# Routing and the last down products of a four-stage layer stack on one core: choice on logits, down products by tile, routing interleaved

## What is computed

```python
logits = x @ gate_w.T                        # [2048, 64]
probs = softmax(logits)
w, sel = top_k(probs, 8); w = w / sum(w)
pos = rank of the token among those that chose the same expert, in order of tokens
valid = pos < 128                            # at most 128 rows for an expert
out = silu(rows @ wg) * (rows @ wu) @ wd     # for each expert, on its rows
y[token] += w * out                          # for valid choices
```

## Time and profile before

| | us |
|---|---|
| three runs | 1732.64, 1737.85, 1740.98 |
| their median | 1737.85 |
| the profiled execution | 1744.28 |
| its span, from the first to the last instruction | 1742.4 |
| outside its span | 1.9 |
| TensorE busy in the span | 1506.9 (86%) |
| VectorE busy | 1062.9 (61%) |
| ScalarE busy | 583.2 (33%) |
| POOL busy | 794.6 (46%) |

### The profile page before, as it was taken

The page is one execution under the profiler, slowest core; times in us unless marked ns, Lnnn a source line. Parts: engine busy times, 40 slices in busy tenths (PEclk is TensorE's granted clock), DMA queues, the critical chain, the costliest instruction groups (busy, mean ns, idle before and its releaser), DMA issues. The chain is left out here.

```text
span 1742.4 us, 19092 instructions
## 1 busy us (share of the span) xinstructions
PE 1506.9 (86%) x5792; PEld 1038.0 (60%) x5792; DVE 1062.9 (61%) x1591; ACT 583.2 (33%) x1034; POOL 794.6 (46%) x491
## 2 busy tenths in 40 slices
PE   6989966899948899988999899999991799998992
PEld 2444323577736677766887787778771455554551
DVE  4887688887898987889988746452553122222220
ACT  4434633344534335343433322121210232222220
POOL 3467853354744445634644326662376232222222
PEclk8999988999969999999999999999995899999996
DMA  6899663356644677766655468997760799999987
GB/s 202 251 280 277 194 217 132 101 156 196 199 140 149 201 221 222 216 192 225 187 183 169 145 201 305 351 317 227 227 191 25 227 329 317 311 306 301 307 211 126
DMA packets 193541, 380.41 MB, mean 218 GB/s; under 512 B 20994, under 2 KB 95106, under 8 KB 192944
## 3 DMA queue, kind: packets, MB, share of 16 engines
q1 hardware_dynamic: 165360, 322.89, 59.8%
q0 software_dynamic: 20032, 39.92, 9.7%
q10 hardware_dynamic: 8064, 16.55, 2.8%
HBM read 301.65 MB, written 124.35 MB: 244 GB/s over the span
## 5 line engine op out<-in xcount | busy, mean ns | idle before, releaser
L1453 POOL TENSOR_TENSOR y<-y,hc 128x2048 f32<-128x2048 f32 x64 | 293.3, 4582 | 250.3 <-DVE hc L1295 250.3
L590 PE MATMUL bank<-tokT,ring 128*128 128x512 f32 x768 | 307.9, 401 | 12.9 <-DVE xall L1150 6.9
L1277 DVE TENSOR_TENSOR_SCAN bx<-bank,state,bx 128x512 f32<-128x512 f32 x256 | 312.6, 1267 | 0.8
L592 PE MATMUL bank<-tokT,ring 128*128 128x512 f32 x768 | 302.3, 394 | 0.0
L591 PE MATMUL bank<-tokT,ring 128*128 128x512 f32 x768 | 302.2, 393 | 0.0
L940 ACT ACTIVATE bank<-dl,an 128x512 f32<-128x512 f32 x256 | 171.0, 684 | 330.4 <-DVE bx L1277 330.3
L1459 POOL TENSOR_TENSOR act<-th,act 128x512 fp32r<-128x512 f32 x96 | 126.4, 1316 | 269.6 <-ACT act L864 269.1
L819 PE MATMUL bank<-wgu,xeT 128*128 128x384 f32 x512 | 181.0, 498 | 0.0
L590 PEld LDWEIGHTS bank<-tokT,ring 128*128 128x128 f32 x768 | 146.2, 190 | 49.2 <-issue 17.6
L602 PE MATMUL bank<-ring,act 128*128 128x512 f32 x360 | 147.6, 410 | 22.6 <-DVE th L1139 17.3
L592 PEld LDWEIGHTS bank<-tokT,ring 128*128 128x128 f32 x768 | 146.0, 190 | 32.1
(11 more groups left out here) (147 smaller groups left out, 2007.9 us busy)
## 6 DMA issues: line engine op xcount, KB each, us to landing
ring<-w_all SPq DMA_DIRECT2D x288, 512.0 KB
wgu<-wgu_in SPq DMA_DIRECT2D x64, 768.0 KB
wde<-wd_in SPq DMA_DIRECT2D x64, 384.0 KB
slots<-empty_in SPq DMA_DIRECT2D x16, 1154.0 KB, 8.7
w_all<-staged_u SPq DMA_DIRECT2D x64, 256.0 KB, 3.2
xe<-slots ACTq DMA_DIRECT2D x56, 288.5 KB
w_all<-fst SPq DMA_DIRECT2D x48, 256.0 KB, 3.7
w_all<-staged_d SPq DMA_DIRECT2D x32, 256.0 KB, 3.7
```

The costliest lines, as they stand in the source:

```text
L590: nc.tensor.matmul(b[:, :], w[:, k, 0, :], x[:, 0, k, :], start=(k == 0), stop=False)
L592: last = nc.tensor.matmul(b[:, :], w[:, k, 1, :], x[:, 0, k, :], start=False, stop=(k == KT - 1))
L1277: nc.vector.tensor_tensor_scan(bx[:, k, :], dA[k % 2][:, :], bx[:, k, :], state[:, k, n:n + 1], ALU.mult, ALU.add).then_inc(S_sc, 1)
L1453: nc.gpsimd.tensor_tensor(y[c % 2][:, :, :], y[c % 2][:, :, :], hc[:, :, :], ALU.add).then_inc(S_ya, 1)
```

## The change

It consists of five edits.

1. **Choice on logits.** VectorE takes the 8 largest logits (`max`), negates the first of them for the exp's bias, replaces the 8 in a copy by a very small number, and makes the mask from that, first in bf16 for the place product (which now waits for step 4 instead of 10). ScalarE makes two exps: of the 8 chosen logits with their sum, and of all 64. The weight is exp x (1 / sum) x mask in one instruction. The key of a slot is position + first slot + 2,000,000 for a chosen expert, with 1,000,000 more where the expert is full, so that one `max` and one subtraction give the slot numbers; `RS` is 14.
2. **Low half of the last mixer on VectorE** instead of POOL, two positions after the up quantum as before.
3. **Held weights.** The down weights of blocks 0 and 1 go to a buffer `held` of their own (over `spr`), loaded by SP at TURN+14 after the last transposes of the mixer. They leave the ring, so the six ring buffers end with blocks 2 to 7, and the last of these loads waits for the last up quantum.
4. **Down products by tile.** `tail(t, js)` does all 8 blocks for one tile, so `TAIL` is two positions earlier, and routing and scatters of tiles 8 to 11 are one position earlier (`base+5` for the scatters of tiles 0 to 11).
5. **The tail is written out** on each engine: the routing of a tile stands between two halves of the products of the next, and POOL's roots stand between scatters.

```diff
             with ExitStack() as last_products:
+                held = sb(last_products, "held", [P, 2, 2 * D], f32r)
-            RS = 17
+            RS = 14
...
+            HELD = M1 - RING
+            quanta = [q for q in quanta if q not in [(len(HALVES) - 1, "down", j) for j in range(HELD)]]
...
-            TAIL_FROM = M1 - RING
-            TAIL = TURN + 12 + 2 * M1 + TAIL_FROM
+            TAIL = TURN + 12 + 2 * M1
...
-            route_at = [DRAIN + 12 + 5 * i for i in range(EARLY)] + [TURN + 13 + 4 * i for i in range(TT)] + [TAIL + 1 + i for i in range(TT)]
+            route_at = [DRAIN + 12 + 5 * i for i in range(EARLY)] + [TURN + 12 + 4 * i for i in range(TT)]
...
                         if pos == TURN + 14:
+                            sp.wait_ge(n3.tp, TT * NCH)
+                            for j in range(HELD):
+                                sp.dma_start(held[:, j, :].bitcast(fp32), a["w_all"][3 * tile_of(len(HALVES) - 1, j) + 2]).then_inc(S_held, 16)
                             load_weights(4, 4)
...
-                    def tail(t):
+                    def tail(t, js):
...
-                        for j in range(TAIL_FROM, M1):
-                            w = ring_ready((h, "down", j)).rearrange("p (s h) -> p s h", s=2)
+                        for j in js:
+                            if j < HELD:
+                                pe.wait_ge(S_held, 16 * HELD)
+                                w = held[:, j, :]
+                            else:
+                                w = ring_ready((h, "down", j))
...
                     def place(i):
-                        pe.wait_ge(S_r, RS * i + 10)
+                        pe.wait_ge(S_r, RS * i + 4)
...
+                    first_part, second_part = range(M1 // 2), range(M1 // 2, M1)
+                    place(11)
+                    tail(0, range(M1))
+                    tail(1, first_part)
+                    route_T(12)
+                    tail(1, second_part)
+                    logits(12)
+                    tail(2, first_part)
+                    place(12)
+                    route_T(13)
+                    tail(2, second_part)
+                    logits(13)
+                    tail(3, first_part)
+                    place(13)
+                    route_T(14)
+                    tail(3, second_part)
+                    logits(14)
+                    route_T(15)
+                    place(14)
+                    logits(15)
+                    place(15)
...
-                        nc.scalar.activation(rt[:, 0, :], HB[2][:, 0:E], ACT.Exp, bias=rc[:, 1:2], accum_out=rc[:, 2:3]).then_inc(S_ex, 1)
+                        nc.scalar.activation(rt[:, 6, 0:TOPK], top8[:, 0, :], ACT.Exp, bias=rc[:, 1:2], accum_out=rc[:, 2:3])
+                        act.wait_ge(S_r, RS * i + 3)
+                        nc.scalar.activation(rt[:, 0, :], HB[2][:, 0:E], ACT.Exp, bias=rc[:, 1:2]).then_inc(S_ex, 1)
...
+                    def gated_lo(h, j):
...
+                        dve.wait_ge(S_gt, i + 1)
+                        dve.wait_ge(S_ah, i + 1)
+                        nc.vector.tensor_tensor(act8[:, 1, j, :], th[:, i % 2, :], act8[:, 0, j, :].bitcast(fp32),
+                                                ALU.subtract).then_inc(S_al, 1)
...
                             dve.wait_ge(S_lg, i + 1)
+                            nc.vector.max(top8[:, 0, :], logit).then_inc(S_r, 1)
                             after(1)
+                            nc.vector.tensor_scalar(rc[:, 1:2], top8[:, 0, 0:1], -1.0, None, ALU.mult).then_inc(S_r, 1)
+                            nc.vector.match_replace(rest, top8[:, 0, :], logit, TAKEN).then_inc(S_r, 1)
+                            after(3)
+                            nc.vector.tensor_scalar(chosen_b[:, :], rest, TAKEN / 2, None, ALU.is_lt).then_inc(S_r, 1)
+                            nc.vector.tensor_scalar(chosen, rest, TAKEN / 2, None, ALU.is_lt).then_inc(S_r, 1)
+                            after(5)
+                            nc.vector.tensor_tensor(first, chosen, first_slot[:, :], ALU.mult).then_inc(S_r, 1)
+                            nc.vector.tensor_copy(r[:, ROW - 1:ROW], number[:, :]).then_inc(S_r, 1)
+                            dve.wait_ge(S_ex, i + 1)
+                            nc.vector.reciprocal(rc[:, 3:4], rc[:, 2:3]).then_inc(S_r, 1)
+                            after(8)
+                            nc.vector.scalar_tensor_tensor(out=r[:, D:D + E], in0=rt[:, 0, :], scalar=rc[:, 3:4], in1=chosen,
+                                                           op0=ALU.mult, op1=ALU.mult).then_inc(S_r, 1)
                         else:
+                            dve.wait_ge(S_pm, i + 1)
+                            nc.vector.tensor_tensor(key, position, first, ALU.add).then_inc(S_r, 1)
+                            nc.vector.tensor_scalar(far, position, float(CAP), FAR, ALU.is_ge, ALU.mult).then_inc(S_r, 1)
+                            after(11)
+                            nc.vector.tensor_tensor(key, key, far, ALU.add).then_inc(S_r, 1)
+                            after(12)
+                            nc.vector.max(top8[:, 1, :], key).then_inc(S_r, 1)
+                            after(13)
+                            nc.vector.tensor_scalar(idx[:, i % SLOTS, :], top8[:, 1, :], -BASE, None, ALU.add).then_inc(S_r, 1)
...
+                    def finished(i):
+                        if i >= 3 * TT:
+                            down_added(len(HALVES) - 1, [i % TT])
+                        dve.wait_ge(S_de, TT * x3_half[i // TT] + i % TT + 1)
+                        stats(n4, i % TT, xall[:, i // TT])
...
+                    side(TAIL)
+                    route(11, 2)
+                    side(TAIL + 1)
+                    finished(12)
+                    route(12, 0)
+                    finished(13)
+                    route(12, 1)
+                    route(13, 0)
+                    route(12, 2)
+                    finished(14)
+                    route(13, 1)
+                    route(14, 0)
+                    route(13, 2)
+                    finished(15)
+                    route(14, 1)
+                    route(15, 0)
+                    route(14, 2)
+                    route(15, 1)
+                    route(15, 2)
...
-                            if kind == "up":
+                            if kind == "up" and h < len(HALVES) - 1:
                                 gated_lo(h, j)
...
+                    for k in range(3):
+                        rows_out(11, k)
+                    rstd(12)
+                    for k in range(3, TOPK):
+                        rows_out(11, k)
+                    rstd(13)
+                    rows_out(12, 0)
+                    rows_out(12, 1)
+                    rstd(14)
+                    for k in range(2, TOPK):
+                        rows_out(12, k)
+                    rstd(15)
+                    for i in range(13, 16):
+                        for k in range(TOPK):
+                            rows_out(i, k)
```

More of the change, by code:

```diff
@@ L30 @@
 FAR = 1.0e6
+BASE = 2.0e6
+TAKEN = -3.0e38
 EPS = 1e-5
@@ L1047, in _ @@
                         states(c)
-                    for pos in range(DRAIN, LAST):
+                    for pos in range(DRAIN, TAIL):
                         side(pos)
@@ L1183, in side @@
                                 down_added(h)
+                        for h, kind, j in quanta_at.get(pos - 2, ()):
+                            if h == len(HALVES) - 1 and kind == "up":
+                                gated_lo(h, j)
                     def split_x_lo(c, b):
@@ L1303, in route @@
                         r = row[:, i % SLOTS, :]
-                        pr, rest, chosen, key, v = (rt[:, j, :] for j in range(1, 6))
+                        rest, chosen, first, key, far = (rt[:, j, :] for j in range(1, 6))
+                        logit, position = HB[2][:, 0:E], HB[3][:, 0:E]
                         def after(s):
-                            dve.wait_ge(S_const, 1)
                             dve.wait_ge(S_r, RS * i + s)
@@ L1346, in route @@
-                            nc.vector.scalar_tensor_tensor(out=v, in0=HB[3][:, 0:E], scalar=float(CAP), in1=chosen,
-                                                           op0=ALU.is_lt, op1=ALU.mult).then_inc(S_r, 1)
-                            after(13)
-                            nc.vector.tensor_tensor(key, key, v, ALU.mult).then_inc(S_r, 1)
-                            after(14)
-                            nc.vector.max(top8[:, 1, :], key).then_inc(S_r, 1)
-                            after(15)
@@ L1353, in route @@
-                            nc.vector.tensor_scalar(top8[:, 2, :], top8[:, 1, :], 0.0, FAR, ALU.is_equal, ALU.mult).then_inc(S_r, 1)
-                            after(16)
-                            nc.vector.scalar_tensor_tensor(out=idx[:, i % SLOTS, :], in0=top8[:, 1, :], scalar=-1.0, in1=top8[:, 2, :],
```

(2 more changed lines are left out.)

92 lines of the change are left out of this document (41 added, 51 removed).

## The result

The changed kernel takes 1721.33 us (median of 6 runs, 1717.19 to 1724.62), the kernel before 1735.94 in the same comparison. The ratio is 0.9915, interval 0.9891 to 0.9938: 14.6 us or 0.85% faster, by the prediction's bound of 0.5% a gain. One of the six runs of before took 5255.45 us; the median of the other five is 1734.03, and the gain by it 12.7. The profiled executions differ by more, 1744.28 against 1721.55. To see why, I cut each span at four events: the first logits (tile 0), the first down product of the last mixer (the T of the prediction), the first scatter of tile 12, and the load of expert rows. "Stage" is from the first logits to that load, which is all that the change touches; "tail" is from T to the load.

A forecast was written before the change was run, and what follows sets the result against it. TensorE's place waits bound the routing, tile 12's slot numbers and then POOL's scatter rate the tail. Part 1's -10.6 and Parts 2 to 4's -11.5 made -22.1 us, so 1716 us against the median, range 1708 to 1729.

The forecast's parts named there:

- Part 1: Routing, choice on logits: all 11.0 us of TensorE's place waits go, 0.4 given back, -10.6 us.
- Part 2: Last mixer, low half on VectorE: POOL no longer falls behind; VectorE's 8 x 0.68 us covered by idle time.
- Part 3: Held down weights: no ring wait; the last down block's load lands at 3.9 us, needed at 4.9.
- Part 4: Tail's down products by tile: last scatter ends 62.1 us after the last up product; Parts 2 to 4 -11.5 us.
- The sum: Whole kernel: -10.6 and -11.5 added to -22.1 us, 1716 us against the median.
- A late semaphore falls into the chain: Rival, between the last up product and tile 12's first scatter: a late release is uncovered; 1722 to 1725 us, chance 0.10.
- DMA: Rival, early routing stretch: DMA binds once TensorE's waits are gone; 1720 to 1725 us, chance 0.15.
- Port exclusion: Rival, routing beside scatters: VectorE steps and scatters exclude each other, 6.9 us a tile; 1747 us, chance 0.05.
- Load to end: From the load of expert rows to the end: 386 us, its length independent of when it starts.

The follow-up runs named there:

- place_late: Changed kernel with the place product waiting for step 9 (weights in the row) instead of step 4 (mask); ratio to before 0.9880.
- after_third: Changed kernel, unchanged file, profiled a third time; 1713.6 us, ratio to before 0.9870.
- low_on_pool: Changed kernel with the low half of the last mixer back on POOL; 1724.85 us, ratio to before 0.9919.
- choice_only: Kernel before with the choice on logits alone added; 1728.28 us, ratio to before 0.9934.
- after_again: Changed kernel, unchanged file, profiled a second time; ratio to before 0.9905.
- runs_broken: Changed kernel with a one-column addition on POOL behind every second scatter of tiles 8 to 11; ratio to before 0.9876.
- tail_only: Changed kernel with the routing of the kernel before and the low half on POOL; ratio to before 0.9942.

## Why the prediction was right, and where it was not

The forecast was 1716 us (22.1 less), the result 1721.3 and 14.6 less; the direction and the range (1708 to 1729) hold.

- **Part 1 (-10.6)** is right in kind and under-sized: -12.3 to -12.6 to T where nothing takes it back, since a stand costs more than its wait. The earlier release alone gave nothing (place_late). In the changed kernel's own profile only 7.0 were left at T: late deliveries, through late rows and the clock behind them, gave back most of the rest.
- **Part 2 (no cost, an end to the backlog)** was right in what it said of the two engines, and its cost of nothing is still the term that failed in two of three profiles. The backlog went: tile 10's last scatter ends at T + 1.9 in after_third and at T + 5.4 in low_on_pool, and the tail is 62.8 against 66.0. The cover on VectorE held: without late deliveries T comes at 225.5 with 0.2 us of waits on the row, and in choice_only, with the subtractions on POOL, at 225.2. What the part had at nothing is what the subtractions did among POOL's scatters. Without them rows of six and more stand in the last mixer, and late deliveries in five of six profiles: alone the part costs 12.2 us, about all of it by late deliveries. On top of the other parts it saves 5.2 us (293.4 to 288.2, on two chips) without them, 0.2 the wrong way (293.6) on the chip of low_on_pool, and costs 2.3 (295.7) in the first profile. A late row costs TensorE more than the stand, as it may then run at 0.66 to 0.72 of its clock.
- **Part 3 (no cost)** held without late deliveries: no ring wait. With them the last load is issued 2.5 us late and TensorE stands 1.3 and 0.97 us.
- **Part 4 (T + 62.1 for parts 2 to 4)** measured T + 63.6, 65.6 and 61.6. The terms in after_again that are over: the last ring load 1.0, the root behind a scatter 1.1 (add to root 3.9 us against 2.8), the clock 1.6; the second stand of 1.0 did not come.
- **The sum** treated the parts as additive. They overlap by 5.7 us between part 1 and parts 3 and 4.
- **Rivals.** "A late semaphore falls into the chain" (1722 to 1725, chance 0.10) is what two of the three profiles of the changed kernel show, in the mixer as well as in the tail, with medians of 1721.3 and 1723.3 (14.6 and 15.5 less than before). It deserved more; the earlier trace rows had shown 8.7 us of it. The third comparison, without late deliveries, gained 25.3, so the forecast of 22.1 lies between what was measured with and without them, and which of the two a chip would show was in no term of it. DMA did not bind. Port exclusion did not come: the mask (L1377) and the moved subtraction (L1191) beside scatters (count, ns min, median, max):

Line views of the changed kernel (count, ns min/median/max):

```profile
L1377 DVE TENSOR_SCALAR chosen_b<-rt x16: 194/195/584, 1046.1 to 1313.1; 128x64 bf16<-128x64 f32 x16
...
L1191 DVE TENSOR_TENSOR act<-th,act x8: 680/684/684, 1229.6 to 1279.3; 128x512 fp32r<-128x512 f32 x8
```

The mask's median stays at 0.195, at most 0.34 beside a scatter and 0.58 beside a subtraction of POOL; the moved subtraction takes 0.684 in all eight, five of them beside a scatter, and no scatter takes over 1.45. By the rule on the shared port pair of "SBUF — State Buffer" in the Trainium skill scatters might have been blocked by it; these rows show no such wait of 0.5 us a step, on which that rival was priced.
- **Load to end.** I took 386 us as fixed. It is 378 to 387 in 14 profiles, so 6 us of the profiled difference were luck on top of a stage that gave less.

## What to carry to other kernels

Before you take a step off an engine, cost both sides: who waits for the new engine's next result, and what the step did in the old engine's order. Here the idle share of VectorE was cover enough, 5.4 us for about nothing, while POOL's scatters without the subtractions between them went with late deliveries that cost 12 us in one kernel. When an engine is late, look first at whether it was busy or stood for a release whose product had long ended. A stall of TensorE of some 2 us can also cost what follows, so price it with the clock. When parts are to be added up, run each alone and all together, and compare the stage that they touch, between two events of the trace; what lies around it varied here by 9 to 11 us, as much as most of the parts are worth.

## What the runs showed of the hardware

- Semaphore deliveries of TensorE, 0.03 us as a rule, came 0.5 to 5.4 us late to SP, VectorE and ScalarE, several of them at once, and 8.9 us late once in before, all while POOL was in a row of six or more indirect DMAs: 20 of 51 ring loads in such rows, none of 1021 elsewhere, and none in the four profiles of one chip. The cause is open.
- TensorE stood 1.88 (runs_broken), 2.03, 2.46, 2.67, 3.21 and 4.37 us, and its granted clock was then 0.50 to 0.72 over the next 4.5 to 5.6 us. After stands of 1.86 (before), 1.91 and 2.23 (tail_only) and 2.00 us (place_late), and after all of 0.7 to 1.3 us that I looked at, it stayed at full. What tells them apart is open.
- One core moved 367 GB/s over 105 us beside a fully busy TensorE without a wait.
